# Turning four tiles of x by 16-bit transposing DMAs instead of on TensorE, with GpSimd splitting and interleaving the halves

## The chip, the cores and the metric

The kernel runs on one core of a Trainium2 chip. The metric is the device time of one execution in microseconds (us), lower is better. An engine here is one of TensorE (PE), VectorE (DVE), ScalarE (ACT), GpSimd (POOL) and SyncE (SP), which issues most transfers.

## The reference

Two graph layers over N = 1250 nodes with D = 512 features each, and a layer norm behind each of them. The graph has 21250 edges, sorted by destination.

```python
edge_index = stack([src, dst])
# first layer: hidden width 1024
agg = segment_sum(x[src], dst)
h = (1 + eps) * x + agg                       # called h0 below
h = relu(batch_norm(h @ W1 + b1))
h = relu(batch_norm(h @ W2 + b2))
x = layernorm(x + (x + h))
# second layer: hidden width 256
h = relu(x @ V1 + c1) @ V2 + c2
x = layernorm(x + h + segment_sum(h[dst], src))
```

All arrays are float32.

## The kernel before

The sum over edges is done as a matrix product with the adjacency counts A. x lies in SBUF as ten tiles of 128 rows (`xs[:, k, :]`, the last has 98 rows). A transposed copy `xT` (features on the partitions, nodes along the free dimension) is needed too, since `h0` is made with features on the partitions: `h0 = eps1 * xT + agg`. Large products are made exact enough by splitting each float32 operand in a high and a low part (`xh` and `xl` of x, `h0h` and `h0l` of h0, `wh` and `wl` of a weight).

**The stages around the change.** The transposed adjacency `AT` is built in NG = 25 groups of 50 destination nodes. For each group g, VectorE writes two sets of one-hot rows (`one_hots(g)`: `hot_s` with 1280 and `hot_k` with 500 bfloat16 elements per partition, each by comparing two operands that lie in SBUF), TensorE multiplies them (`build(g)`, ten small matmuls), and ScalarE copies the result from PSUM to `AT` (`group_out(g)`). The one-hot tiles have two buffers each: `one_hots(g)` waits until `build(g-2)` is done, and `build(g)` waits for `one_hots(g)` and for `group_out(g-2)`.

The nodes are aggregated in three chunks of columns, `CH = [(0, 250), (250, 750), (750, 1250)]`, which are complete behind groups 5, 15 and 25. From group 5 on TensorE does, in each slot g, `build(g)` and then four units of aggregation (`aggregate(i, k)`: two matmuls, of `xh` and `xl` of tile k). Slots 5 to 14 take chunk 0 (250 columns, one tile k = g - 5 in each slot), slots 15 to 24 take chunk 1 (500 columns), and chunk 2 follows as a tail. Tables set what else is done in a slot: `high_at` and `low_at` say behind which group `xh` (ScalarE) and `xl` (VectorE, `x_low`, again two operands in SBUF) of tiles 5 to 9 are made, `cols_at` says where TensorE turns tiles 7, 8 and 9 of x (`x_cols`: four transposes into a PSUM bank), and `turn_at` where ScalarE copies them to `xT` (`x_turn`). Tiles 5 and 6 are turned earlier, behind `build(2)` and `build(4)` (`early_cols`). `h0_own(i)` on VectorE adds `eps1 * xT` to the sums in PSUM, `h0_high` on ScalarE and `h0_low` on VectorE split the result.

GpSimd has nothing to do between the indirect loads at the start and the end of group 24. Then it makes the low parts of W1 (`wl`), which TensorE needs in the next stage, z = W1 h0. SyncE loads x, then W1, and then waits with the next transfers (`turns`, the spilled adjacency) for work behind group 24.

Later in the program the same machinery as in the change is used at another place: ScalarE writes the low and the high 16 bits of `xT` to two int16 planes, SyncE turns each of them by a transposing DMA (`plane_T<-planes`, 128x1280), and ScalarE and GpSimd write them back interleaved (`rows_back`).

Of the kernel before, what the change touches and what calls it, by code (L numbers as in the profile page):

```python
# [23 lines left out]
def gnn_kernel(nc, x, src, dst, eps, w1, b1, g1, be1, w2, b2, g2, be2, lw1, lb1, lw2, lb2, out, a_spill):  # L24
# [38 lines left out]
    with ctx:  # L63
# [116 lines left out]
        par_r = tmp("par_r", [P, P], F32)  # L180

# [72 lines left out]
        pads_set, bounds_set = sem("pads_set"), sem("bounds_set")  # L254
        rows_T, ln_var, ln_std_s, ln_aff, x1_last_set, x1_set = (
# [91 lines left out]
        cols_at = {6: half + 2, 7: half + 3, 11: half + 4}  # L347
        turn_at = {6: half + 2, 7: half + 3, 12: half + 4}
        high_at = {5: half, 8: half + 1, 9: half + 2, 10: half + 3, 11: half + 4}
        low_at = {7: half, 10: half + 1, 11: half + 2, 12: half + 3, 13: half + 4}  # L350
        early_cols = {EARLY - 3: half, EARLY - 1: half + 1}
        w1_at = {CHG[1] + t: t for t in range(HT)}
        assert EARLY == half and NT == half + 5 and max(cols_at) < CHG[1] and CHG[1] + HT <= NG and 2 + DT <= x_bank(half)
# [24 lines left out]
        def _(sp):  # L378
# [12 lines left out]
            for d in range(DT):  # L391
                sp.dma_start(w1s[:, :, d * P:d * P + P], w1[d * P:d * P + P, :].rearrange("p (t c) -> p t c", c=P)
                             ).then_inc(w1_in, 16)
            sp.wait_ge(pad_set, ATS)
# [42 lines left out]
        def _(pl):  # L437
# [25 lines left out]
            for t in half_out:  # L463
                nc.gpsimd.memset(t[:, N:COLS], 0).then_inc(pad_set, 1)
            pl.wait_ge(rowsel, 1)
# [9 lines left out]
            nc.gpsimd.memset(asked[0:1, :], 0.0).then_inc(runs_asked, 1)  # L475

# [77 lines left out]
        def _(act):  # L554
# [26 lines left out]
            def w1_high(t):  # L581
                if t == 0:
                    act.wait_ge(w1_in, 16 * DT)
                    act.wait_ge(xl_set, NT)
                    act.wait_ge(x_turned, NT)
                nc.scalar.activation(wh[:, t, :], w1s[:, t, :], ACT.Copy).then_inc(w1h_set, 1)
# [24 lines left out]
            with act.If(bad == 0):  # L611
                for g in range(EARLY, NG):
                    group_out(g)
                    if g in turn_at:
                        x_turn(turn_at[g])
# [9 lines left out]
            with act.Else():  # L625
                for k in turn_at.values():
                    x_turn(k)
# [168 lines left out]
        def _(v):  # L796
# [59 lines left out]
            def h0_own(i):  # L856
# [3 lines left out]
                if i == 0:  # L860
                    v.wait_ge(xT_set, NT)
# [4 lines left out]
            def h0_low(i):  # L866
                c, d = divmod(i, DT)
                c0, c1 = CH[c]
                v.wait_ge(h0h_set, i + 1)
                nc.vector.tensor_tensor(h0l[c][:, d, :], ps[:, 2 + i % 6, 0:c1 - c0],  # L870
# [276 lines left out]
        def _(pe):  # L1147
# [56 lines left out]
            def aggregate(i, k):  # L1204
# [3 lines left out]
                if k == 0:  # L1208
# [3 lines left out]
                    elif i >= DT:  # L1212
                        pe.wait_ge(xT_set, NT)
# [21 lines left out]
            with pe.If(bad == 0):  # L1235
                for g in range(EARLY, NG):
# [6 lines left out]
                    if g in cols_at:  # L1243
                        x_cols(cols_at[g])
            with pe.Else():
                for k in cols_at.values():
                    x_cols(k)
                pe.wait_ge(xT_set, NT)
# [173 lines left out]
```

## Time and profile before

| | |
|---|---|
| median of 3 runs | 249.57 us (249.5 to 250.74) |
| the profiled execution's own time | 249.95 us |
| its span from first to last instruction | 248.1 us |
| granted TensorE clock, mean | 0.995 |
| PE busy | 231.0 us (93%) |
| DVE busy | 156.2 us (63%) |
| ACT busy | 134.2 us (54%) |
| POOL busy | 88.0 us (35%) |

The span leaves 1.85 us of the execution's own time outside. Busy times are shares of the whole span; an engine can be idle on average and still be the one that is waited for in a stage.

### The profile page before, as it was taken

The page shows a single profiled execution, that of the slowest core. Times are in us where ns is not written, and L with a number is a line of the kernel's source. Part 1 is how long each engine was busy: PE and PEld are TensorE (multiplying, and loading weights), DVE is VectorE, ACT ScalarE, POOL GpSimd, SP SyncE. Part 2 cuts the span into 40 slices and gives each one's busy share as a digit, 9 for nine tenths or more (in the row PEclk, how much of TensorE's full clock was granted, in tenths as well). Part 3 has the DMA queues.
Part 4 walks back from the last instruction along what each step waited for, and adds up shares of the span by engine and source line. Part 5 has one row for each costly group of instructions (what it writes and reads, how often), then busy time and mean ns, then how long its engine had stood idle before and what let it go on. Part 6 is the DMA issues. An engine that isn't in the chain of part 4 may idle for free.

```text
span 248.1 us, 3897 instructions
## 1 busy us (share of the span) xinstructions
PE 231.0 (93%) x1454; PEld 197.3 (80%) x1454; DVE 156.2 (63%) x362; ACT 134.2 (54%) x233; POOL 88.0 (35%) x83
## 2 busy tenths in 40 slices
PE   0858999999999999999999999999999999999990
PEld 0845997777888888888888888888889997888970
DVE  1669899873966344555544316264876899796374
ACT  0656774763868067444455504457471639936373
POOL 5420000004920006565554500423456459701251
PEclk9999999999999999999999999999999999999998
DMA  3467800000066501111000087503209920000334
GB/s 100 156 214 214 202 0 3 1 3 3 3 261 239 198 1 45 42 42 45 0 0 0 4 206 142 106 3 60 45 4 170 202 85 3 0 0 0 131 127 160
DMA packets 32323, 19.96 MB, mean 80 GB/s; under 512 B 21927, under 2 KB 27084, under 8 KB 32302
## 3 DMA queue, kind: packets, MB, share of 16 engines
q1 hardware_dynamic: 31796, 19.45, 28.6%
q8 instruction: 13, 0.21, 0.4%
q0 software_dynamic: 160, 0.13, 0.2%
q10 hardware_dynamic: 346, 0.10, 0.2%
q14 instruction: 8, 0.07, 0.1%
HBM read 8.51 MB, written 5.92 MB: 58 GB/s over the span
## 4 chain that ended last, share of the span: by engine, by line
PE 70%; DVE 12%; DMA 7%; ACT 6%; issue 2%; POOL 1%; SPq 1%; DVEq 0%
PE ps L1281 22%; PE ps L1220 17%; PE ps L1298 11%; PE ps L1344 9%; PE ps L1362 6%; PE ps L1311 3%; DVE hot_s L849 3%; DMA plane_T<-planes 2%; PE ps L1200 2%; DMA src_i<-in_src 2%; DVE xT L984 2%; DMA pairs<-pair 2%; ACT planes L715 1%; DVE small_t L942 1%; DMA run<-pairs,start_i 1%
## 5 line engine op out<-in xcount | busy, mean ns | idle before, releaser
L942 DVE BATCH_NORM_STATS2 small_t<-ps 128x6 f32<-128x500 f32 (+1 forms) x36 | 21.6, 599 | 38.7 <-PE ps L1281 25.2
L1220 PE MATMUL ps<-AT,xh 128*128 128x500 f32 (+2 forms) x120 | 42.6, 366 | 0.4 <-ACT AT L569 0.4
L1220 PE MATMUL ps<-AT,xl 128*128 128x500 f32 (+2 forms) x120 | 40.9, 352 | 0.0
L1281 PE MATMUL ps<-h0h,wh 128*128 128x500 f32 (+1 forms) x96 | 33.9, 353 | 0.0
L1281 PE MATMUL ps<-h0h,wl 128*128 128x500 f32 (+1 forms) x96 | 33.9, 353 | 0.0
L1281 PE MATMUL ps<-h0l,wh 128*128 128x500 f32 (+1 forms) x96 | 33.8, 352 | 0.0
L485 POOL TENSOR_TENSOR wl<-w2s,wh 128x512 fp32r<-128x512 f32 x8 | 11.1, 1384 | 43.9 <-ACT wh L689 43.9
L480 POOL TENSOR_TENSOR wl<-w1s,wh 128x512 fp32r<-128x512 f32 x8 | 10.1, 1301 | 45.7 <-ACT AT L569 45.7
L1220 PEld LDWEIGHTS ps<-AT,xh 128*128 128x128 f32 (+1 forms) x120 | 22.6, 188 | 3.3 <-ACT AT L569 0.6
L1220 PEld LDWEIGHTS ps<-AT,xl 128*128 128x128 f32 (+1 forms) x120 | 22.7, 189 | 2.7
L1298 PE MATMUL ps<-a1h,wh 128*128 128x500 f32 (+1 forms) x96 | 23.7, 355 | 0.0
L1298 PE MATMUL ps<-a1h,wl 128*128 128x500 f32 (+1 forms) x96 | 23.5, 353 | 0.0
L1298 PE MATMUL ps<-a1l,wh 128*128 128x500 f32 (+1 forms) x96 | 23.4, 353 | 0.0
L569 ACT ACTIVATE AT<-ps 128x500 fp32r<-128x500 f32 x25 | 14.8, 590 | 15.6 <-PE ps L1200 15.6
L849 DVE TENSOR_TENSOR hot_s<-iota,loT 128x1280 bf16<-128x1280 bf16 x25 | 20.5, 820 | 2.3 <-PE ps L1200 2.2
L1344 PE MATMUL ps<-A,uh 128*128 128x512 f32 (+3 forms) x60 | 20.5, 357 | 0.0
L1281 PEld LDWEIGHTS ps<-h0h,wh 128*128 128x128 f32 x96 | 18.1, 188 | 2.9 <-issue 0.4
L1344 PE MATMUL ps<-A,ul 128*128 128x512 f32 (+3 forms) x60 | 20.3, 354 | 0.0
L1281 PEld LDWEIGHTS ps<-h0l,wh 128*128 128x128 f32 x96 | 18.0, 188 | 2.5
L1281 PEld LDWEIGHTS ps<-h0h,wl 128*128 128x128 f32 x96 | 18.0, 188 | 2.4
L489 POOL TENSOR_TENSOR a1l<-a,a1h 128x1250 fp32r<-128x1250 f32 x7 | 18.8, 2682 | 0.0
L663 ACT ACTIVATE small_t<-small_t 128x1 f32<-128x1 f32 x12 | 3.5, 295 | 27.7 <-DVE small_t L943 27.7
(148 smaller groups left out, 508.2 us busy)
## 6 DMA issues: line engine op xcount, KB each, us to landing
turns<-half_out SPq DMA_DIRECT2D x10, 320.0 KB, 2.2
out<-x SPq DMA_DIRECT2D x9, 256.0 KB
w1s<-in_L_gnn_W SPq DMA_DIRECT2D x4, 512.0 KB, 7.1
w2s<-in_L_gnn_W SPq DMA_DIRECT2D x8, 256.0 KB, 2.7
xs<-in_x SPq DMA_DIRECT2D x1, 1280.0 KB, 7.9
xs<-in_x SPq DMA_DIRECT2D x1, 1024.0 KB
lws<-in_L_gnn_W SPq DMA_DIRECT2D x1, 512.0 KB, 4.0
lw2s<-in_L_gnn_W SPq DMA_DIRECT2D x1, 512.0 KB, 4.2
```

Source lines behind the costliest of these rows:

```text
L480: nc.gpsimd.tensor_tensor(wl[:, t, :], w1s[:, t, :], wh[:, t, :].bitcast(F32), ALU.subtract).then_inc(w1l_set, 1)
L485: nc.gpsimd.tensor_tensor(wl[:, t, :], w2s[t % W2R][:, :], wh[:, t, :].bitcast(F32), ALU.subtract).then_inc(w2l_set, 1)
L489: nc.gpsimd.tensor_tensor(a1(a1l, t), a32[t % 2][:, :], a1(a1h, t).bitcast(F32), ALU.subtract).then_inc(a1l_set, 1)
L569: nc.scalar.activation(AT[:, :, g * WG * WIN:(g + 1) * WG * WIN].rearrange("p k (w d) -> p k w d", w=WG), ps[:, g % 2, 0:GCOLS].rearrange( ...
L849: nc.vector.tensor_tensor(hot_s[g % 2][:, :, :, :], iota2[:, None, :, :].broadcast_to([P, WG, P, 2]), loT[:, w, None, :].broadcast_to([P, ...
L942: link(nc.vector.bn_stats(stats[:, 6 * c:6 * c + 6], ps[:, zbank(t, c), 0:c1 - c0]))
L1220: last = mm(o, part[0:r, k, d * P:d * P + P], AT[0:r, k, c0:c1], start=(k == 0 and j == 0), stop=(k == NT - 1 and j == 1))
L1281: last = mm(ps[:, zbank(t, c), 0:c1 - c0], w[:, t, d * P:d * P + P], h[c][:, d, :], start=(d == 0 and j == 0), stop=(d == DT - 1 and j == 2))
L1298: last = mm(ps[:, zbank(t, c), 0:c1 - c0], w[:, k, (t - HT) * P:(t - HT + 1) * P], a1(a, k)[:, c0:c1], start=(k == 0 and j == 0), stop=(k ...
L1311: last = mm(u_at(k), x[:, d, P * k:P * k + r], w[:, d, :], start=(d == 0 and j == 0 and k % 2 == 0), stop=(d == DT - 1 and j == 2), skip_g ...
L1344: last = mm(v_at(i, m), (uh, ul)[j][0:r, k, m * P:m * P + P], a_rows(k)[0:r, c0:c1], start=(k == 0 and j == 0 and (m == 0 or v_banks[i][0] ...
L1362: last = mm(ps[0:r, y_banks[k % len(y_banks)], :], part[:, f:f + r], w[:, m, :], start=(m == 0 and j == 0), stop=(m == LT - 1 and j == 2))
```

## The change

Tile 5 is still turned on TensorE behind `build(2)`. Tiles 6 to 9 (XD = 6) are no longer turned on TensorE nor copied by ScalarE. Instead, GpSimd waits until group 10 is copied to `AT` (`AT_set` 11) and then copies the low and the high 16 bits of each float of tiles 6 to 8 (128x1536 int16 each) and of tile 9 (98x512 each) to two planes. SyncE issues two transposing DMAs from these planes (16 blocks of 128x128 each), SBUF to SBUF. GpSimd then interleaves the turned halves into `xT` in eight copies, two for each tile. The first `h0_own` of chunk 2 waits for them. The planes and their turned copies lie in 16 KB where `h0h` and `h0l` of chunks 1 and 2 are written later, so the last `h0_low` of chunk 1 waits for the DMAs, and ScalarE's write of `wh` tile 4, which lies over x tile 6, waits for the planes.

```diff
@@ the new tiles
+        XD = NT // 2 + 1
+        x_plane = [at(f"x_plane{i}", [P, NT - XD, D], I16, R_XD + i * (NT - XD) * XTILE) for i in range(2)]
+        x_plane_T = [at(f"x_plane_T{i}", [P, (NT - XD) * DT, P], I16, R_XD + (2 + i) * (NT - XD) * XTILE) for i in range(2)]
@@ the tables
-        cols_at = {6: half + 2, 7: half + 3, 11: half + 4}
-        turn_at = {6: half + 2, 7: half + 3, 12: half + 4}
+        x_parts = [(k0, k1, i) for k0, k1 in ((XD, NT - 1), (NT - 1, NT)) for i in range(2)]
+        PLANES_AT = 11
-        early_cols = {EARLY - 3: half, EARLY - 1: half + 1}
+        early_cols = {EARLY - 3: half}
@@ SyncE, behind the loads of W1
+            sp.wait_ge(x_plane_set, len(x_parts))
+            for i in range(2):
+                sp.dma_start_transpose(x_plane_T[i][:, :, :], x_plane[i][:, :, :].rearrange("p t d -> p (t d)")
+                                       ).then_inc(x_planes_T, 16)
@@ GpSimd, at its start
+            for t in x_plane:
+                nc.gpsimd.memset(t[:, NT - 1 - XD, :], 0).then_inc(x_pad, 1)
@@ GpSimd, ahead of its wait for group 24
+            def x_to_plane(k0, k1, i):
+                r = rows[k1 - 1]
+                nc.gpsimd.tensor_copy(x_plane[i][0:r, k0 - XD:k1 - XD, :], half_of(xs[0:r, k0:k1, :].rearrange(
+                    "p t d -> p (t d)"), i).rearrange("p (t d) -> p t d", d=D)).then_inc(x_plane_set, 1)
+
+            def x_late(k0, k1, i):
+                c0, c1 = P * k0, min(P * k1, N)
+                for k in range(k0, k1):
+                    r = rows[k]
+                    src = x_plane_T[i][:, (k - XD) * DT:(k - XD + 1) * DT, 0:r]
+                    out = xT[:, :, P * k:P * k + r].bitcast(I16).rearrange("p d (c i) -> p d c i", i=2)[:, :, :, i]
+                    last = nc.gpsimd.tensor_copy(out, src)
+                last.then_inc(xT_late, 1)
+
+            pl.wait_ge(x_in2, 32)
+            pl.wait_ge(x_pad, 2)
+            pl.wait_ge(AT_set, PLANES_AT)
+            for part in x_parts:
+                x_to_plane(*part)
+            for part in x_parts:
+                pl.wait_ge(x_planes_T, 32)
+                x_late(*part)
@@ ScalarE, in w1_high and behind group_out
-                    act.wait_ge(x_turned, NT)
+                    act.wait_ge(x_turned, XD)
+                if t == XD - X_UNDER_W1:
+                    act.wait_ge(x_plane_set, len(x_parts))
-                    if g in turn_at:
-                        x_turn(turn_at[g])
@@ VectorE, in h0_own and h0_low
-                    v.wait_ge(xT_set, NT)
+                    v.wait_ge(xT_set, XD)
+                if i == NI - DT:
+                    v.wait_ge(xT_late, len(x_parts))
+                if i == NI - DT - 1:
+                    v.wait_ge(x_planes_T, 32)
@@ TensorE
-                        pe.wait_ge(xT_set, NT)
+                        pe.wait_ge(xT_set, XD)
-                    if g in cols_at:
-                        x_cols(cols_at[g])
```

On TensorE the transposes stood between the aggregation of a slot and the next build. These are its rows in slots 6 and 7, before:

```order
L1220 MATMUL ps<-AT,xh 128x250
L1220 MATMUL ps<-AT,xl 128x250
L1162 MATMUL ps<-ident,xs 128x128 [waits xT_set,x_in2]
L1162 MATMUL ps<-ident,xs 128x128 x3
L1200 MATMUL ps<-hot_k_72,hot_s_70 128x50 [waits AT_set,hot]
L1200 MATMUL ps<-hot_k_72,hot_s_70 128x50 x9
L1220 MATMUL ps<-AT,xh 128x250 [waits xl_set]
```

And the same place of TensorE now:

```order
L1262 MATMUL ps<-AT,xh 128x250
L1262 MATMUL ps<-AT,xl 128x250
L1242 MATMUL ps<-hot_k_72,hot_s_70 128x50 [waits AT_set,hot]
L1242 MATMUL ps<-hot_k_72,hot_s_70 128x50 x9
L1262 MATMUL ps<-AT,xh 128x250 [waits xl_set]
```

Four transposes are gone here, and so they are behind the build of group 4, in slot 7 and in slot 11; each build follows the aggregation at once.

On GpSimd, between its last memset of the start and the first low part of W2, there stood before:

```order
L472 DMA run_113<-pairs,start_i_111 125x128 [waits start_set]
L475 MEMSET small_t 1x1
L480 TENSOR_TENSOR wl<-w1s,wh 128x512 [waits w1h_set,AT_set]
L480 TENSOR_TENSOR wl<-w1s,wh 128x512 [waits w1h_set] x7
L485 TENSOR_TENSOR wl<-w2s_53,wh 128x512 [waits w2h_set]
```

And now:

```order
L491 MEMSET small_t 1x1
L495 COPY x_plane_119<-xs 128x1536 [waits AT_set,x_pad,x_in2]
L495 COPY x_plane_120<-xs 128x1536
L495 COPY x_plane_119<-xs 98x512
L495 COPY x_plane_120<-xs 98x512
L504 COPY xT<-x_plane_T_121 128x4x128 [waits x_planes_T]
L504 COPY xT<-x_plane_T_121 128x4x128 x2
L504 COPY xT<-x_plane_T_122 128x4x128 [waits x_planes_T]
L504 COPY xT<-x_plane_T_122 128x4x128 x2
L504 COPY xT<-x_plane_T_121 128x4x98 [waits x_planes_T]
L504 COPY xT<-x_plane_T_122 128x4x98 [waits x_planes_T]
L519 TENSOR_TENSOR wl<-w1s,wh 128x512 [waits w1h_set,AT_set]
```

Twelve copies that read SBUF stand where GpSimd was idle; the low parts of W1 come behind them.

## Rows read from the trace of the kernel before

**Rows 1.** Windows of 7 and 21 us: busy us (instructions) of each engine, clock, DMA.

```profile
31.00:38.00 7.00, 6.74 (x93) 6.27 (x93) 7.00 (x13) 4.54 (x10) 0.00 (x0) 1.00 0.00 0
38.00:59.00 21.00, 21.00 (x182) 16.47 (x182) 16.47 (x33) 12.17 (x25) 0.00 (x0) 1.00 0.01 2
```

**Rows 2.** Chain that ended last, slots 5 to 14: start, us, what.

```profile
23.89 0.22 issue
...
26.82 0.44 PE ps L1162 x4
...
30.11 0.52 ACT xh L565
...
30.65 0.69 DVE xl L828
31.35 0.73 DVE hot_s L849
32.08 0.33 DVE hot_k L852
32.41 0.60 DVE xl L828
...
37.47 0.43 PE ps L1200 x10
```

**Rows 3.** Timeline: the copy of group 10 to AT, and tile 9's transposes.

```profile
31.88 0.59 ACT L569 ACTIVATE AT<-ps 128x500 fp32r<-128x500 f32 x1 [0.18 <-PE ps L1200]
...
33.99 0.50 PE L1162 MATMUL ps<-ident,xs 98*128 98x98 f32 x4
```

**Rows 4.** Groups by line on POOL: its int16 copies of the later stage.

```profile
L508 POOL COPY xr<-plane_T 128x640 int16<-128x640 int16 x6 | 5.3, 924 | 3.9 <-DMA plane_T<-planes 3.9
```

**Rows 5.** Timeline of POOL and DVE where both read SBUF, and alone.

```profile
168.04 1.21 DVE L994 TENSOR_TENSOR lws<-lws,ps 128x1024 f32<-128x1024 f32 x1
171.75 2.90 POOL L497 TENSOR_TENSOR xpl<-xT,xph 128x1250 fp32r<-128x1250 f32 x1 [8.15 <-ACT xph L706]
172.66 3.08 DVE L999 TENSOR_TENSOR lw1l<-lws,lw1h 128x1024 fp32r<-128x1024 f32 x1 [3.41 <-ACT lw1h L725]
...
67.14 1.34 DVE L963 TENSOR_TENSOR half_out<-half_out,ident 128x128 int16<-128x128 int16 x1
72.50 0.29 DVE L963 TENSOR_TENSOR half_out<-half_out,ident 128x128 int16<-128x128 int16 x1 [0.55 <-ACT half_out L639]
...
208.73 1.66 POOL L523 CAST A<-half_out 128x1250 fp32r<-128x1250 int16 x1
209.31 1.36 DVE L1065 SCALAR_TENSOR_TENSOR ul<-u,uh 128x256 fp32r<-128x256 f32 x1
```

**Rows 6.** The tile plane_T: time of an issue on SP in ns, time to landing.

```profile
L424 SPq DMA_TRANSPOSE plane_T<-planes x6: 1330/1442/1540, 156.8 to 186.2; - x6
...
DMA to landing us min/median/max: 3.5/3.5/5.5
```

**Rows 7.** One-hots of groups 19 and 20 on DVE, and the build of 20.

```profile
43.60 0.82 DVE L849 TENSOR_TENSOR hot_s<-iota,loT 128x1280 bf16<-128x1280 bf16 x1 [0.39 <-PE ps L1200]
...
47.35 0.41 DVE L852 TENSOR_TENSOR hot_k<-iota_k,keyT 128x500 bf16<-128x500 bf16 x1
...
49.81 0.28 PE ps L1200 x10
```

**Rows 8.** Timeline of POOL at the start.

```profile
6.83 1.18 POOL L466 IOTA nodes<- 128x1250 f32 x1 [2.35 <-DVE edge_row L812]
```

**Rows 9.** The low parts of W1 on POOL, and the chain's piece that uses them.

```profile
59.51 10.12 POOL L480 TENSOR_TENSOR wl<-w1s,wh 128x512 fp32r<-128x512 f32 x8 [45.72 <-ACT AT L569]
...
78.92 54.96 PE ps L1281 x288
```

**Rows 10.** Chain: TensorE's last work; and the window in which its clock falls.

```profile
234.07 8.40 PE ps L1362 x36
...
245.00:246.00 1.00, 0.00 (x0) 0.00 (x0) 0.39 (x1) 0.00 (x0) 0.00 (x0) 0.83 0.69 256
```

More of the change, by code:

```diff
@@ L180, in gnn_kernel @@
         par_r = tmp("par_r", [P, P], F32)
+        XD = NT // 2 + 1
+        XTILE = D * 2
+        R_XD = R_W - 4 * (NT - XD) * XTILE
+        x_plane = [at(f"x_plane{i}", [P, NT - XD, D], I16, R_XD + i * (NT - XD) * XTILE) for i in range(2)]
+        x_plane_T = [at(f"x_plane_T{i}", [P, (NT - XD) * DT, P], I16, R_XD + (2 + i) * (NT - XD) * XTILE) for i in range(2)]
+        assert TMP[0] <= R_XD and R_XD % 32 == 0
+        assert R_H0 + DT * (CH[1][0] + CH[1][1]) * 4 + (DT - 1) * (CH[1][1] - CH[1][0]) * 4 <= R_XD
+        assert R_H0 + 2 * DT * CH[2][0] * 4 <= R_XD + 2 * (NT - XD) * XTILE
         ident = misc("ident", [P, P], F32)
@@ L254, in gnn_kernel @@
         pads_set, bounds_set = sem("pads_set"), sem("bounds_set")
+        x_pad, x_plane_set, x_planes_T, xT_late = (sem(n) for n in ("x_pad", "x_plane_set", "x_planes_T", "xT_late"))
         rows_T, ln_var, ln_std_s, ln_aff, x1_last_set, x1_set = (
@@ L346, in gnn_kernel @@
         EARLY = CHG[0]
-        cols_at = {6: half + 2, 7: half + 3, 11: half + 4}
-        turn_at = {6: half + 2, 7: half + 3, 12: half + 4}
+        x_parts = [(k0, k1, i) for k0, k1 in ((XD, NT - 1), (NT - 1, NT)) for i in range(2)]
+        PLANES_AT = 11
         high_at = {5: half, 8: half + 1, 9: half + 2, 10: half + 3, 11: half + 4}
         low_at = {7: half, 10: half + 1, 11: half + 2, 12: half + 3, 13: half + 4}
-        early_cols = {EARLY - 3: half, EARLY - 1: half + 1}
+        early_cols = {EARLY - 3: half}
         w1_at = {CHG[1] + t: t for t in range(HT)}
-        assert EARLY == half and NT == half + 5 and max(cols_at) < CHG[1] and CHG[1] + HT <= NG and 2 + DT <= x_bank(half)
+        assert EARLY == half and NT == half + 5 and CHG[1] + HT <= NG and 2 + DT <= x_bank(half)
+        assert XD == half + 1 and CH[1][1] <= XD * P
         def h0_after(g):
@@ L625, in _ @@
             with act.Else():
-                for k in turn_at.values():
-                    x_turn(k)
                 for k in high_at.values():
@@ L1242, in _ @@
                         build(g)
-                    if g in cols_at:
-                        x_cols(cols_at[g])
             with pe.Else():
-                for k in cols_at.values():
-                    x_cols(k)
-                pe.wait_ge(xT_set, NT)
+                pe.wait_ge(xT_set, XD)
                 pe.wait_ge(gen_zero, 1)
```

## The prediction

> **What bounds the kernel now.** I read the chain that ended last first, since it says which engine each stretch waits for, and then the windows and timelines of the stretches that the change touches. TensorE holds most of the chain. The stretch in which the transposes stand is the exception. From 30.65 to 37.42 us the chain runs on VectorE alone: xl of a tile, hot_s, hot_k, again and again, at 0.60 to 0.69, 0.73 and 0.33 us apart, until the build of group 14 at 37.47 us can start [rows 2]. In the window from 31 to 38 us VectorE is busy 7.00 of 7.00 us, TensorE 6.74, and GpSimd does nothing [rows 1]. So both engines are nearly full there, and VectorE is the one that ends last. From 38 to 59 us it is the other way: TensorE is busy 21.00 of 21.00 us, VectorE 16.47 [rows 1]. The slots of that stretch take TensorE about 2.2 us each, while two one-hot instructions take VectorE 1.06 us.
>
> **What TensorE saves.** Four tiles are no longer turned. In slot 6 this is 0.44 us of the chain, and slot 7 has the same piece once more [rows 2]; tile 9 in slot 11 has 0.50 us [rows 3], and tile 6 behind group 4 counts as 0.44. That is 1.8 us of TensorE. But a build cannot start ahead of its one-hots, and VectorE's instructions are as many as before. What the saving can move is the start of VectorE's gapless run. It was released by xh of tile 6, which ScalarE made from 30.11 to 30.63 us, behind two copies of turned tiles [rows 2]; I put what VectorE waited for it at 0.1 us. The other place is the 0.22 us of issue at 23.89 us, ahead of the first aggregation [rows 2], where TensorE's sequencer comes from the transposes of tile 6. I take 0.3 us for both. The bounds are 0 and 1.8. ScalarE's four copies that go are not on the chain behind 30.65 us and give nothing more.
>
> **The four plane copies.** They are not in the trace. The nearest row is the same kind of copy, int16 with a step of two on one side, at 128x640: 924 ns [rows 4]; pairs of them take 1.75 us, 0.875 us each from start to start, as the row's busy time of 5.3 us over six also says. In proportion a copy of 1536 elements takes 2.1 us and one of 512 takes 0.7 us, 5.6 us for the four. Group 10 is copied to AT by 32.47 us [rows 3], so they start at about 32.2 us. This is inside VectorE's gapless run, with some 5 us of it to go.
>
> Do the two engines hold each other up? The trace has three kinds of places. At 171.75 us GpSimd works for 2.90 us on two SBUF operands, and a VectorE instruction with two SBUF inputs that starts at 172.66 takes 3.08 us, where one of the same shape with an input from PSUM takes 1.21 [rows 5]. It ends at 175.74, 1.09 us behind GpSimd's end: it did its work only when GpSimd was through. A 16-bit tensor_tensor takes 1.34 us beside GpSimd and 0.29 alone. A GpSimd cast with one input does the same: it ends at 210.39 and the VectorE instruction that started at 209.31 ends at 210.67 [rows 5]. The one-hots and xl all have two SBUF inputs. So each plane copy stops VectorE for nearly its own length. From the first pair, VectorE would have to begin 1.21 us ahead of 175.74, that is 0.12 us before GpSimd's end; I take 0.15 us off each copy: 1.95 + 1.95 + 0.55 + 0.55 = 5.0 us. VectorE has no idle time in the run to put this in, so the build of group 14 and all behind it moves by it. The bounds: 5.9 us if the copies cost in proportion to the 924 ns and hold the whole time, and 0 if GpSimd never gets in (a rival below).
>
> The Trainium skill, "SBUF — State Buffer", section "Who interferes with whom", speaks against this change: a VectorE instruction with two SBUF inputs and a GpSimd instruction that reads SBUF exclude each other, for the whole instruction, and issue order decides who waits. By its whole instruction the four would cost 5.6 us in place of 5.0. The rows above show the exclusion too, and the measured ends put it 0.1 us short of the whole.
>
> **The transposing DMAs.** An issue takes SP 1.44 us for 10 blocks, and its data land 3.5 to 5.5 us behind it [rows 6]. With 16 blocks in proportion: 2.3 us for the first issue, and 5.6 us behind the second; 7 us in all, with 5 and 8 as bounds. Behind the planes, which end at about 38.9 us (32.2, the 5.6 us of copies, and two or three VectorE instructions let in between), they land at about 46 us. SP has nothing else to issue until the adjacency is complete, so nothing is queued behind them.
>
> **The eight interleaving copies.** Six have 512 elements (0.7 us) and two 392 (0.54): 5.3 us, of which by the same 0.15 us they stop VectorE for 4.1. They fall on one-hots of groups 17 to 20. Before, hot_k of group 20 was done at 47.68 us and its build came at 49.81: 2.1 us of slack, and VectorE waited 0.39 us at 43.60 [rows 7], 2.5 us together. All this shifts by the same 4.7 us, so the slack stays. Two of the eight should fall on h0_own or h0_low, which have an operand in PSUM and are not stopped. Six times 0.55 less 2.5 is 0.8; I take 0.7. Bounds: 0 and 4.1 less 2.5, which is 1.6.
>
> **What costs nothing.** The two memsets of 128x512 at the start lie in front of a 2.35 us wait of GpSimd [rows 8]. The low parts of W1 come behind the interleaving; that is through at about 55 us, and the copy of group 24, for which they wait anyway, is at 59 plus the delay. They took 10.12 us from 59.51, and TensorE wants the first at 78.92 [rows 9], 9 us behind the last. The same slack covers h0_own of chunk 2, which waits for xT. ScalarE's wait for the planes stands in slot 19, some 10 us behind them.
>
> **The sum.** -0.3 + 5.0 + 0.7 = +5.4 us, on the profiled execution's 249.95 us: 255.35. The median before is 0.4 us under that execution, and I put the forecast at 255.2. Bounds of the terms: -1.8 to 0, 3.9 (copies a quarter cheaper than in proportion, still holding) to 5.9, 0 to 1.6; together 252.1 to 257.5. I hold the ends to be unlikely at once.
>
> **Rivals.**
> 1. TensorE's clock falls. With the copies in VectorE's way, hot_k of group 12 is done at 32.2 + 1.95 + 0.60 + 1.95 + 0.73 + 0.55 + 0.33 = 38.3 us, while TensorE is through with slot 11 at about 33.4: 4.9 us idle in one piece. At the end of the program TensorE's last work ends at 242.47, and the granted clock, 0.83 in the second from 245 on [rows 10], falls there from 2.4 to 1.2 GHz at about 245.66, after 3.2 us of idling. For: the gap is longer. Against: it is one gap, in a stretch that VectorE bounds. A slot of 1.3 us would take 2.6 against VectorE's 1.66, so 0.95 us lost in each of slots 12 to 14 at most, of which the wait hides the first: up to 1.5 us more, 255.5 to 256.8.
> 2. GpSimd is kept out, and the kernel is not slower. VectorE's instructions in the run overlap (820 ns long, 0.73 apart), and no row shows GpSimd getting in between two such. If it waits for VectorE's first idle time, that is at 43.60 us [rows 7], in TensorE's stretch: each copy then takes from a slack of 2 to 3 us and VectorE catches up before the next, the planes turn at about 57, xT is complete at about 70, and TensorE loses nothing or the tail waits up to 1 us: 249.6 to 250.7. It decides if the first plane copy ends behind 40 us. The rows where GpSimd stops VectorE are all ones in which GpSimd was there first.
> 3. These operands don't exclude each other, and only the saving is left: 249.65, or as little as 248.2 with all of TensorE's 1.8 us. The 16-bit and the one-input rows speak against it.
> 4. The reading with a step costs more than the writing with one, planes and interleaving half as dear again: 2.8 us more from the planes and up to 1.2 from the rest, 257 to 259. Nothing in the trace reads so.
>
> **How the numbers follow.** The forecast has 0.47, the clock 0.22, GpSimd kept out 0.15, no exclusion 0.07, dearer copies 0.09. Without the last rival's upper half, no exclusion and half of the case in which GpSimd is kept out, 0.8 is left: 250.2 to 258.4. A change of 0.5% (1.25 us) is about what a measurement can tell from none. Slower by more: 0.47 + 0.22 + 0.09 and nothing of the rest, 0.78. Faster by more: a part of the third rival, 0.04. Within: 0.18.
>
> **What the new profile would show.** Right: VectorE instructions of 2.0 to 2.8 us between 32 and 39 us where they were 0.4 to 0.8, the build of group 14 at 42 us, TensorE idle for 4 to 5 us in one piece at about 33 to 38, the transposes landed at about 46, no wait for xT or for wl. Wrong: a first plane copy that itself takes over 5 us (kept out), or hot_s staying at 0.82 us beside a plane copy. What I could have most wrong is the price of the copies, on which both positive terms of the sum hang.

## The result and the profile after

The changed kernel takes 251.25 us (median, 250.79 to 251.86) where the kernel before took 249.79 beside it: ratio 1.0052, 95% interval 1.0040 to 1.0065, or 1.3 us more. The forecast was 5.4 us more. The profiled execution took 251.40 us.

First GpSimd's timeline of the changed kernel:

```profile
32.68 11.67 POOL L495 COPY x_plane<-xs 128x1536 int16<-128x1536 int16 x4 [19.00 <-ACT AT L608]
51.96 7.01 POOL L504 COPY xT<-x_plane_T 128x512 int16<-128x512 int16 x8 [7.61 <-DMA x_plane_T<-x_plane]
60.31 10.10 POOL L519 TENSOR_TENSOR wl<-w1s,wh 128x512 fp32r<-128x512 f32 x8 [1.34 <-ACT AT L608]
```

VectorE's timeline of the same stretch:

```profile
37.51 0.81 DVE L887 TENSOR_TENSOR hot_s<-iota,loT 128x1280 bf16<-128x1280 bf16 x1
...
39.31 0.41 DVE L890 TENSOR_TENSOR hot_k<-iota_k,keyT 128x500 bf16<-128x500 bf16 x1
39.64 1.62 DVE L903 SCALAR_TENSOR_TENSOR ps<-xT,small_t,ps 128x250 f32<-128x250 f32 x4
41.19 1.95 DVE L887 TENSOR_TENSOR hot_s<-iota,loT 128x1280 bf16<-128x1280 bf16 x1
43.06 0.82 DVE L890 TENSOR_TENSOR hot_k<-iota_k,keyT 128x500 bf16<-128x500 bf16 x1
43.80 1.23 DVE L887 TENSOR_TENSOR hot_s<-iota,loT 128x1280 bf16<-128x1280 bf16 x1
```

The row of line 495, the plane copies, with the shortest, median and longest in ns:

```profile
L495 POOL COPY x_plane<-xs x4: 794/1330/8364, 32.7 to 43.6; 128x1536 int16<-128x1536 int16 x2, 98x512 int16<-98x512 int16 x2
```

The first plane copy "takes" 8.36 us, from 32.68 to 41.04, and the second 1.85. For 7 us the first did nothing: VectorE's one-hots keep their 0.81 and 0.41 us, and 12 of its instructions begin behind 32.68 and ahead of 39.64. It ends only when VectorE has come to `h0_own` (39.64), which has an operand in PSUM. The one-hots behind that become longer, but in the stretch where VectorE has slack [rows 1, 7].

The windows of the changed kernel, in the columns of [rows 1]:

```profile
31.00:38.00 7.00, 6.44 (x89) 5.76 (x87) 7.00 (x13) 4.12 (x8) 5.32 (x1) 1.00 0.01 2
38.00:45.00 7.00, 6.53 (x62) 5.22 (x59) 7.00 (x12) 3.40 (x7) 6.35 (x4) 1.00 0.01 2
45.00:60.00 15.00, 15.00 (x127) 11.58 (x126) 13.16 (x23) 9.02 (x19) 7.01 (x8) 1.00 0.44 72
...
79.00:90.00 11.00, 10.56 (x59) 8.91 (x58) 5.75 (x13) 3.50 (x7) 0.00 (x0) 1.00 0.54 185
```

TensorE loses 0.47 us at one build, at 43.93 (first line below), and nothing from 45 to 60 us, where the eight interleaving copies lie. But it stands again at 84.28 us, in the next stage, which no step of the prediction looked at. TensorE's waits in its timeline:

```profile
43.93 0.43 PE L1242 MATMUL ps<-hot_k,hot_s 128*128 128x50 bf16 x10 [0.47 <-DVE hot_k L890]
84.28 0.50 PE L1319 MATMUL ps<-h0h,wh 128*128 128x500 f32 x1 [0.43 <-DVE h0l L912]
```

ScalarE's timeline ahead of the second:

```profile
73.16 1.24 ACT L677 ACTIVATE half_out<-AT 128x1250 int16<-128x1250 f32 x1
...
75.57 1.25 ACT L677 ACTIVATE half_out<-AT 128x1250 int16<-128x1250 f32 x1 [1.08 <-DMA turns<-half_out]
76.72 0.18 ACT L677 ACTIVATION_READ_ACCUMULATOR half_out<-AT 128x1 f32 x1
76.81 0.57 ACT L635 ACTIVATE h0h<-ps 128x500 fp32r<-128x500 f32 x1
```

Behind group 24 ScalarE copies the ten tiles of counts to four buffers `half_out`, from which SyncE sends them to `turns`. The seventh copy reuses the third buffer and waits 1.08 us for the third transfer. Behind it on ScalarE stand `h0_high` of the second slice of chunk 2, the last three copies and `h0_high` of the third slice; VectorE and ScalarE then do the fourth slice, and TensorE waits for its `h0_low`. The chain says the same:

```profile
70.98 4.57 DMA turns<-half_out
75.55 0.02 issue
75.57 1.34 ACT half_out L677 x2
76.91 0.47 ACT h0h L635
77.38 3.68 ACT half_out L677 x6
81.06 0.48 ACT h0h L635
...
83.55 0.69 DVE h0l L912
...
84.28 51.10 PE ps L1319 x264
```

The row of `turns` gives its landing (min/median/max) as 2.2/4.2/5.5 us in the changed kernel; a second profile of the kernel before (e15) has 2.2/3.4/5.3 and no such wait. The change touches none of this code.

A part of what two profiles differ by is not the change. In e15, the kernel before again, TensorE's granted clock was 0.50 from 18 to 22 us and 0.78 from 22 to 24, where its first profile had 1.00, and group 24's aggregation began at 59.14 instead of 58.80. The changed kernel's profile had such a stretch too (0.50 from 22 to 24) and began it at 59.60. So 0.3 of the 0.8 us by which it looks late there is no more than two profiles of one kernel differ by. That the clock makes this difference is not shown: e9 (below), with a clock of 0.50 from 20 to 22, began its last build at 58.77, and e16, with full clock, at 58.97.

### The profile page after: what moved, and what is told of

It is laid out like the page before. It is cut to its first block, busy times and chain, and to the rows that moved or that the text cites. A ratio compares the mean times of both kernels' runs of the same rounds, so it can differ in the third digit from the quotient of the medians.

```text
span 249.5 us, 3876 instructions
## 1 busy us (share of the span) xinstructions
PE 231.2 (93%) x1438; PEld 196.6 (79%) x1438; DVE 160.4 (64%) x362; ACT 132.4 (53%) x229; POOL 107.4 (43%) x97
## 4 chain that ended last, share of the span: by engine, by line
PE 70%; DVE 15%; DMA 7%; ACT 5%; issue 2%; POOL 1%; SPq 0%; DVEq 0%; ACTq 0%
PE ps L1336 22%; PE ps L1319 20%; PE ps L1382 9%; PE ps L1262 7%; PE ps L1400 6%; DVE hot_s L887 5%; PE ps L1349 3%; DVE hot_k L890 2%; ACT half_out L677 2%; DMA turns<-half_out 2%; DMA src_i<-in_src 2%; DVE gains L1000 2%; PE ps L1242 2%; DMA pairs<-pair 2%; DMA run<-pairs,start_i 1%
## 5 line engine op out<-in xcount | busy, mean ns | idle before, releaser
L887 DVE TENSOR_TENSOR hot_s<-iota,loT 128x1280 bf16<-128x1280 bf16 x25 | 22.2, 888 | 1.2 <-PE ps L1242 1.1
L495 POOL COPY x_plane<-xs 128x1536 int16<-128x1536 int16 (+1 forms) x4 | 11.7, 2955 | 19.0 <-ACT AT L608 19.0
```

The lines of the kernel that those rows point to most:

```text
L495: nc.gpsimd.tensor_copy(x_plane[i][0:r, k0 - XD:k1 - XD, :], half_of(xs[0:r, k0:k1, :].rearrange("p t d -> p (t d)"), i).rearrange("p (t d ...
L887: nc.vector.tensor_tensor(hot_s[g % 2][:, :, :, :], iota2[:, None, :, :].broadcast_to([P, WG, P, 2]), loT[:, w, None, :].broadcast_to([P, ...
```

## The experiments

Ratios are to the kernel before on the same chip, with 95% intervals; 0.0010 is 0.25 us.

**e1, the saving alone.**

```diff
-    (wait for xs and AT; x_to_plane x4; x_late x4 on GpSimd; both transposing DMAs on SyncE)
+    nc.gpsimd.memset(xT[:, :, P * XD:N], 0.0).then_inc(xT_late, len(x_parts))
```

The waits of ScalarE and VectorE for the planes and the DMAs are left out with them.

> The changed kernel with its plane copies, both transposing DMAs and the eight interleaving copies left out: tiles 6 to 9 of xT are filled with zeros by one early GpSimd memset, so the output is not the reference's. It shows what TensorE and ScalarE save by themselves. By the forecast's first term 0.3 us less than before (249.5). A rival: the stretch up to the build of group 14 goes by VectorE alone, and the saving is nothing (249.8). A second rival: TensorE's emptier start lets its clock fall between 20 and 24 us, as in the profile of the changed kernel, and the time is 0.3 us above before (250.1).

Measured: 251.53 us, 1.0056 (1.0041 to 1.0071). With no plane, no DMA and no interleaving the whole loss is there. But the substitute disturbed the run; GpSimd's timeline of e1:

```profile
13.27 1.73 POOL L503 MEMSET xT<- 128x1928 f32 x1
```

VectorE's:

```profile
13.70 1.38 DVE L863 TENSOR_SCALAR rel<-run,small_t 125x128 f32<-125x128 f32 x1 [0.35 <-DMA run<-pairs,start_i]
```

In the kernel before this `rel` takes 0.29 us. The clearing held it, and the groups began 0.6 us late. ScalarE waited 0.80 for `turns` here too.

**e2, the additions alone.** TensorE and ScalarE turn all ten tiles again (`cols_at`, `turn_at`, `early_cols` of before restored), GpSimd and SyncE do their new work as well. The interleaving also waits for ScalarE's copies to `xT`, and ScalarE, VectorE and TensorE wait for ten turned tiles again. The main lines:

```diff
-        early_cols = {EARLY - 3: half}
+        early_cols = {EARLY - 3: half, EARLY - 1: half + 1}
+                    if g in turn_at: x_turn(turn_at[g])      # ScalarE
+                    if g in cols_at: x_cols(cols_at[g])      # TensorE
```

> All ten tiles are turned on TensorE as before, and GpSimd and SyncE do the plane copies, the DMAs and the interleaving of the changed kernel on top (the same values are written to xT once more). If the added part is what costs, this stands 1 to 1.5 us above before (250.8 to 251.3), the first plane copy ends at about 41 to 42 us and the build of group 17 comes some 0.6 us late. If the loss comes from what was taken off TensorE (its clock, its emptier slots), this is as fast as before (249.8). By the forecast's mechanism (each copy gets in at the next boundary) it would be above 254.

Measured: 254.53 us, 1.0189 (1.0165 to 1.0214). Here the planes got in at once. GpSimd's timeline of e2:

```profile
33.03 5.46 POOL L497 COPY x_plane<-xs 128x1536 int16<-128x1536 int16 x4 [19.33 <-ACT AT L611]
45.50 8.15 POOL L506 COPY xT<-x_plane_T 128x512 int16<-128x512 int16 x8 [7.01 <-DMA x_plane_T<-x_plane]
```

VectorE's:

```profile
33.33 2.08 DVE L893 TENSOR_TENSOR hot_s<-iota,loT 128x1280 bf16<-128x1280 bf16 x1
35.33 1.67 DVE L896 TENSOR_TENSOR hot_k<-iota_k,keyT 128x500 bf16<-128x500 bf16 x1
36.93 1.09 DVE L872 TENSOR_TENSOR xl<-xs,xh 128x512 fp32r<-128x512 f32 x1
37.95 1.23 DVE L893 TENSOR_TENSOR hot_s<-iota,loT 128x1280 bf16<-128x1280 bf16 x1
```

Against 0.82, 0.41, 0.68 and 0.81 undisturbed they are 1.26, 1.26, 0.41 and 0.42 longer, 3.35 us for the four copies. Group 24's aggregation began at 62.83, 3.7 behind e15's. There was no wait for `turns`, and the interleaving cost TensorE nothing: 15.00 busy of 15.00 from 45 to 60 us.

**e3, gaps in VectorE's run.** The changed kernel with a memset of two elements behind the one-hots of groups 11 to 14:

```diff
+                    if g in (11, 12, 13, 14):
+                        nc.vector.memset(gap[:, 2 * (g - 11):2 * (g - 11) + 2], 0.0)
```

> The changed kernel with four tiny VectorE memsets (no SBUF input), one behind the one-hots of each of groups 11 to 14. Theory A (an unbroken run of VectorE instructions with two SBUF inputs keeps the shared read port, and GpSimd gets in only at an instruction that does not need it): the first plane copy now ends at about 34 to 36 us in place of 41, the others follow at the next memsets, VectorE's one-hots behind them are stretched by 1 to 2 us, the build of group 14 comes at 40 to 42 us, and the time is 253 to 255. Theory B (the first copy's 8.4 us are its own cost, the engines don't exclude each other): the first copy still takes 8.4 us and the time stays at 251.2 to 251.6.

Measured: 254.71 us, 1.0179 (1.0153 to 1.0206). VectorE's timeline of e3, and GpSimd's:

```profile
32.43 0.06 DVE L929 MEMSET gap<- 128x2 f32 x1
33.01 2.09 DVE L888 TENSOR_TENSOR hot_s<-iota,loT 128x1280 bf16<-128x1280 bf16 x1
...
32.57 5.62 POOL L496 COPY x_plane<-xs 128x1536 int16<-128x1536 int16 x4 [18.80 <-ACT AT L609]
```

By its row the first memset was over 0.08 us before the plane copy came, and the copy got in at the next boundary; the pattern is that of e2. ScalarE waited 0.8 for `turns` here, so not all of the time belongs to the planes. The plane copies are the lever, and a break in VectorE's run just ahead of them lets them in.

**e4, planes behind group 19.** `PLANES_AT = 19`.

> The changed kernel with the planes behind group 18 instead of group 10 (PLANES_AT 19), so from about 47 us on, where TensorE is the bound and VectorE has idle time and 2 to 3 us of slack. Theory A: the copies get in at once, take some 6 us in all, no build waits for them, the transposed planes land at about 60 and the interleaving is through by 68 us, ahead of what waits for it: 249.8 to 250.3, the loss of 0.6 us at group 17 is gone. Theory B (a first copy of 8.4 us by its own cost): planes done at about 58, interleaving at about 75, h0_own of the last chunk and the low parts of W1 late, 251 to 254.

Measured: 250.72 us, 1.0029 (1.0015 to 1.0042), lower than the changed kernel but above before, and a miss for the 249.8 to 250.3 of theory A. The copies got in at once, but one build waited 0.53 for its one-hots at 50.53. The interleaving now lies at 59.16 to 64.5 and pushes `wl` to 64.42, the packet of e9 below passed at 73.0, and TensorE waited 1.21 at 85.14.

**e5 and e8, the order of the copies,** in the kernel before and in the changed one:

```diff
-        halves = [range(0, 4), range(4, 7), range(7, NT), range(0)]
+        halves = [range(0, 4), range(4, 6), range(6, NT), range(0)]
```

> The kernel before with one edit: the copies of the counts of tiles to half_out are split 4, 2, 4, 0 between the four high parts of chunk 2 instead of 4, 3, 3, 0, so that the seventh copy, which has to wait for the third transfer to turns, stands behind h0_high of the second slice and no longer ahead of it. In the kernel before, that copy waits for nothing, so both theories expect no change here, 249.5 to 250.1: it is the control for e8. If it is faster or slower by more than 0.4, the order itself has a price, and e8 has to be read against it.

> The changed kernel with the edit of e5. There the seventh copy waits 1.08 for the third transfer to turns, h0_high of the second slice of chunk 2 stands behind it, and TensorE waits 0.43 for h0_low. Theory C: with the high part ahead of the copy TensorE no longer waits there: 0.4 to 0.7 less than the changed kernel, 250.5 to 250.9. Rival E: the wait is covered by TensorE's queue or comes back one slice later at the eighth copy: 251.1 to 251.4.

Measured: e5 250.25 us, 0.9996 (0.9983 to 1.0009), nothing. e8 250.52 us, 1.0012 (0.9999 to 1.0026), 1.0 less than the changed kernel by the ratios. ScalarE still waits for `turns`, 0.39, but nobody behind it does: TensorE is busy 11.00 of 11.00 from 79 to 90 us. So the wait was worth 0.5 to 1.0 us of the 1.3 (this run and e9).

**e6 and e7, the saving with the clearing elsewhere.** In e6 the memset stands behind `AT_set` of group 24, ahead of `wl`; in e7 moreover tile 6 is turned on TensorE, and only tiles 7 to 9 are cleared (from `P * (XD + 1)` on):

```diff
+            pl.wait_ge(AT_set, NG)
+            nc.gpsimd.memset(xT[:, :, P * XD:N], 0.0).then_inc(xT_late, len(x_parts))
-        early_cols = {EARLY - 3: half}
+        early_cols = {EARLY - 3: half, EARLY - 1: half + 1}      # e7 only
```

> As e1 (TensorE no longer turns tiles 6 to 9 and nothing takes the work over; xT of tiles 6 to 9 is only cleared), but GpSimd's clearing of xT stands behind group 24, ahead of wl, instead of ahead of the planes at 13.3. Theory C: the 1.4 of e1 come from leaving the transposes out (later start of the run of VectorE behind the gap of TensorE, and the wait for turns in ScalarE's seventh copy): 251.0 to 251.6 again. Rival D: the early clearing held up VectorE, and e1 overstated it: then 249.6 to 250.5, and the 1.3 of the whole change come from the planes and the interleaving after all.

> As e6, but TensorE and ScalarE turn tile 6 behind build 4 as in the kernel before; tiles 7 to 9 alone are left out. It asks which of the transposes was worth something to the time. If the gap of TensorE behind build 4 and its clock at 20 to 24 carry the loss, this is back at 249.5 to 250.2. If the loss comes from the transposes inside the slots of groups 6, 7 and 11 (their saving lets the rest run ahead, into transfers that land late), it stays with e6, near 251.3.

Measured: e6 251.34 us, 1.0047 (1.0028 to 1.0066); e7 251.38, 1.0041 (1.0022 to 1.0060). They can't be read as intended. The memset pushed `wl` back by 1.7 us in e6 and by 1.3 in e7, onto more of VectorE's int16 additions to `half_out` (three took 3.96 and 3.94 us where the changed kernel's took 2.83), the packet of e9 below passed late in both (70.5 and 72.0), and TensorE waited 1.22 and 0.39 behind them. Their ratios differ by less than their intervals, so they show nothing of tile 6 either.

**e9 and e10, code that is not executed.** What e1, e4, e8 and the changed kernel share against before, e2 and e5 is the time at which a packet of instructions passes. The queues in the DMA view of the changed kernel from 72.5 to 73.0 us (packets, MB, share of 16 engines):

```profile
q1 hardware_dynamic: 75, 0.19, 95.4%
q8 instruction: 1, 0.02, 15.6%
```

The same view of e15 from 64.5 to 65.0:

```profile
DMA packets 1, 0.02 MB, mean 33 GB/s; under 512 B 0, under 2 KB 0, under 8 KB 0
...
q8 instruction: 1, 0.02, 16.3%
```

15.6% of 16 engines for 0.5 us is one engine held for 1.25 us, among transfers that keep all the others busy. In e15 it passes 4 us ahead of the first transfer, alone. The edit puts matmuls in the branch that is not taken:

```diff
             with pe.Else():
+                between(28)      # e9, changed kernel; between(100) in e10, kernel before
```

> The changed kernel with 28 matmuls written into the Else branch of TensorE, which is not taken: nothing more is executed, only the instructions behind the branch lie 56 instructions further on, where they lay in the kernel before (28 transposes left the program, 16 of them executed, 12 in that Else). In the traces a packet of instructions (16 KB, 1.2 to 1.6 on one of the 16 DMA engines) passes at 63.5 to 64.5 in the kernel before and e5 and at 67.5 in e2, ahead of the transfers to turns, but at 72.5 in the changed kernel and at 72 to 73 in e1, e4 and e8, between them, and only there does the third transfer land 4.2 to 4.6 after its issue. Theory F: this packet delays the third transfer, and with it ScalarE's seventh copy (1.08) and TensorE (0.43 and a restart). Then the packet is back near 64, the wait for turns is gone, and the time is 250.3 to 250.8. Rival G: the late landing has another cause (the phase of the transfers against ScalarE's copies): packet moved, wait still there, 251.1 to 251.5.

> The kernel before with 100 matmuls in the Else branch of TensorE, not taken: 200 instructions, so that the packet boundaries behind the branch come 200 instructions earlier, which is 56 short of a whole packet of 256. Nothing else is changed. Theory F: the packet that passed at 93.5 now passes near 72, one of the first transfers to turns lands above 4 after its issue, ScalarE's seventh copy waits 0.5 to 1.1 for it, and the kernel before loses 0.4 to 0.9: 250.5 to 251.0 on this chip if before is 250.1. Rival G: unchanged within 0.2.

Measured: e9 250.74 us, 1.0032 (1.0019 to 1.0044). The packet passed at 64.5, landing was 2.2/3.3/5.2, nobody waited for `turns`, and TensorE was busy 11.00 of 11.00 us from 79 to 90. e10: 252.01 us, 1.0087 (1.0070 to 1.0105), more than theory F gave, and for another reason. The packet came at 73.0, but 4.7 us behind the first transfer, and no copy waited. Instead TensorE stood at the jump; its timeline in e10:

```profile
60.12 0.38 PE L1220 MATMUL ps<-AT,xl 98*128 98x500 f32 x1
61.98 0.47 PE L1220 MATMUL ps<-AT,xh 128*128 128x500 f32 x1 [1.48 <-DVE h0l L870]
```

The same place in e15:

```profile
60.66 0.39 PE L1220 MATMUL ps<-AT,xl 98*128 98x500 f32 x1
60.89 0.39 PE L1220 MATMUL ps<-AT,xh 128*128 128x500 f32 x1
```

The matmul at 61.98 is the first behind the If. The row names `h0l` as releaser, but in e15 the same matmul starts at 60.89, while that `h0l` starts at 61.74. So it did not wait for that `h0l`. That it waited for its instructions is argued only: the packet before the stand came at 59.2 and took about 1.2 us, the next came at 62.5, and none passed during the stand. The other 0.7 of the 2.2 us of e10 stays unplaced.

**e11 and e13, the saving again, padded.** e11 is e1 with `between(28)`; in e13 the clearing moreover waits for the twentieth group:

```diff
+            pl.wait_ge(AT_set, 20)
             nc.gpsimd.memset(xT[:, :, P * XD:N], 0.0).then_inc(xT_late, len(x_parts))
```

> As e1 (transposes of tiles 6 to 9 left out, nothing in their place, xT of these tiles cleared early), with the 28 matmuls of e9 in the Else branch. Theory F: e1's loss of 1.4 was mostly the packet: 0.7 to 1.0 less than e1, 250.4 to 250.8 where before is 250.1; what remains is the later start of VectorE's run. It does not get faster than before by more than 0.3, since VectorE bounds groups 10 to 17 and TensorE's freed time there is slack. Rival G: as e1, 251.5.

> As e11 (transposes of tiles 6 to 9 left out with nothing in their place, xT of these tiles only cleared, 28 matmuls in the Else branch of TensorE), but the clearing stands behind the twentieth group. In e1 and e11 it ran at 13.27 and held VectorE's rel for 1.38 instead of 0.29, so that every group started 0.55 late, and in e6 it pushed wl by 1.7 into VectorE's work on half_out. If the saving by itself is worth nothing but costs nothing (VectorE bounds the groups), this is within 0.3 of before: 249.7 to 250.3 where before is 250.0. If leaving the transposes out has a cost of its own, it stays at 250.7 or more.

Measured: e11 251.12 us, 1.0048 (1.0034 to 1.0063), a miss for theory F: the wait for `turns` was gone, but the groups began 0.8 late behind the early clearing. e13 250.02 us, 0.9990 (0.9981 to 0.9999). Without the early clearing the loss is gone, and the saving is worth 0.25 us, between 0.02 and 0.5; e15, the unchanged kernel measured as one more version, came out at 0.9995.

**e12, an attempt at the best version.** `PLANES_AT = 19`, the split of e8, `between(28)`.

> An attempt at the best version: the changed kernel with PLANES_AT = 19, where VectorE has idle time and TensorE does not wait for it, the split of e8, and the 28 matmuls of e9 in the Else branch. Theories A and F together: the plane copies cost TensorE nothing (group 24 as early as in the kernel before or 0.1 to 0.3 earlier), no wait for turns: 249.6 to 250.3, within 0.3 of before. If it is slower than before by over 0.5, a third cost is still unnamed.

Measured: 251.02 us, 1.0041 (1.0026 to 1.0055), a miss. GpSimd's timeline of e12:

```profile
58.82 5.32 POOL L504 COPY xT<-x_plane_T 128x512 int16<-128x512 int16 x8 [7.14 <-DMA x_plane_T<-x_plane]
64.08 10.24 POOL L519 TENSOR_TENSOR wl<-w1s,wh 128x512 fp32r<-128x512 f32 x8
```

VectorE's:

```profile
66.68 3.93 DVE L1005 TENSOR_TENSOR half_out<-half_out,ident 128x128 int16<-128x128 int16 x3
```

The late planes push the interleaving against `wl` and `wl` onto the additions, as in e6, and one build waits 0.52 at 50.11; TensorE waits 0.36 more at 83.87. No version here beats the kernel before.

**e14, planes earlier, and e15, before again.** e14: `PLANES_AT = 8` and `between(28)`. e15: no edit.

> The changed kernel with PLANES_AT = 8 and the 28 matmuls of e9. GpSimd may begin its first plane copy some 3 us earlier. Theory A (VectorE's unbroken run keeps GpSimd out until its first instruction that reads PSUM, h0_own near 39.5): the copy begins earlier but ends at the same place, 40.5 to 41.2, as one instruction of about 11 to 13, and the time is that of e9 within 0.3. If instead the copy ends early in the run of VectorE, the exclusion depends on who waited first, and the time goes up by 2 to 4 as in e3.

> The kernel before, unchanged, as one more kernel of the comparison: a second profile of it, and a measure of what the comparison calls no difference. Ratio 0.998 to 1.002. TensorE's granted clock may be at half speed somewhere between 19 and 24, as in e5 and e2, or at full speed as in the first profile; if so, the 0.3 to 0.4 by which e5 and the changed kernel start their groups later does not belong to the change.

Measured: e15 250.07 us, 0.9995 (0.9985 to 1.0005). e14 254.09 us, 1.0150 (1.0136 to 1.0165), against theory A: GpSimd came at 28.21 and got in at once, in an unbroken run. VectorE in e14:

```profile
27.52 0.82 DVE L887 TENSOR_TENSOR hot_s<-iota,loT 128x1280 bf16<-128x1280 bf16 x1
28.25 1.69 DVE L890 TENSOR_TENSOR hot_k<-iota_k,keyT 128x500 bf16<-128x500 bf16 x1
29.87 2.08 DVE L887 TENSOR_TENSOR hot_s<-iota,loT 128x1280 bf16<-128x1280 bf16 x1
```

**e16, both remedies:** the split and `between(28)` in the changed kernel.

> The changed kernel with both remedies for the wait for turns, the split of e8 and the 28 matmuls of e9, PLANES_AT as it was. If both only remove the same wait, this is what either gives, 250.3 to 250.8 where before is 250.0; what is left above before then belongs to the plane copies behind 41. If they add up, 249.8 to 250.2.

Measured: 250.85 us, 1.0023 (1.0012 to 1.0033). They don't add up; they remove the same wait.

**e17 and e18, where the copy comes.** Both with `between(28)`; e17 has `PLANES_AT = 10`, e18:

```diff
             pl.wait_ge(AT_set, PLANES_AT)
+            pl.wait_ge(xh_set, half + 4)
```

> The changed kernel with PLANES_AT = 10 and the 28 matmuls of e9. e14 and e2 have refuted theory A as it stood: there GpSimd got in although VectorE's run was unbroken. What the nine traces have in common is where in VectorE's instruction the first plane copy comes: 0.15 to 0.17 behind the start of xl in the changed kernel, e8, e9 and e16 (kept out for 7 us), 0.31 behind it in e2 and 0.69 behind the start of hot_s in e14 (in at the next boundary). Theory H: a copy that comes just behind the start of a VectorE instruction is kept out until the run breaks, one that comes later in it gets in at the next boundary. With PLANES_AT = 10 it comes at about 31.4 minus the 0.2 to 0.4 by which these kernels differ, 0.54 behind the start of xl: in at once under theory H, first copy 1.7 to 2.1, hot_s near 31.4 takes 2.0, and the time is 253.5 to 254.5. Theory A: kept out for 8 us, first copy 9.5 to 10, 250.5 to 250.9.

> The changed kernel with the 28 matmuls of e9, in which GpSimd waits, behind AT of the eleventh group, for the high part of x as well (ScalarE's xh, which ends 0.51 later). The first plane copy then comes at 33.2 minus the same 0.2 to 0.4, some 0.08 behind the start of hot_s. Theory H: just behind the start of an instruction, so it is kept out again until h0_own near 39.3: one copy of 7.5 to 8, 250.5 to 250.9. If it gets in at once here (hot_s or hot_k of 1.7 to 2.1, 254), the place in the instruction does not decide, and why the changed kernel is spared stays open.

Measured: e17 250.49 us, 1.0014 (1.0002 to 1.0026); e18 250.63, 1.0023 (1.0009 to 1.0036). GpSimd's timeline of e17:

```profile
31.68 12.97 POOL L495 COPY x_plane<-xs 128x1536 int16<-128x1536 int16 x4 [17.81 <-ACT AT L608]
```

Of e18:

```profile
32.62 11.16 POOL L495 COPY x_plane<-xs 128x1536 int16<-128x1536 int16 x4 [18.93 <-ACT xh L605]
```

Both were kept out. In e17 the copy came 0.54 behind the start of xl, late in it, so theory H falls; theory A's numbers for e17 came true (a first copy of 9.66 us), though e2 and e14 speak against it as it stood. What fits all nine traces is how long VectorE had then run without a break (a start more than 0.03 us behind the usual distance): 1.3 us in e14, 2.0 in e2, 0.1 in e3 behind its memset, and GpSimd got in; 4.3 us in e17 and 5.6 to 6.2 in the changed kernel, e8, e9, e16 and e18, and it was kept out. That was found in the traces afterwards, and no run was made to test it.

## Why the prediction was wrong, by its steps

**The failed step** is the four plane copies: that each gets in at once and that "VectorE has no idle time in the run to put this in", 5.0 us. They did not get in: the first stood from 32.68 to 41.04, and the four together cost TensorE 0.47 us at one build (0.8 by the ratios, below) in place of 5.0. The second half is right where the copies do get in: e2, e3 and e14 lost 3.75 to 4.7 us. What happened is rival 2, given 0.15: the first copy ended behind the 40 at which the rival said it decides, and both signs that the prediction gave for being wrong came, a first copy of over 5 us and `hot_s` at 0.82 us beside it. The rival's own time, 249.6 to 250.7, was too low for the changed kernel (251.25); it had no wait for `turns` either. That the measured time still lies in the stated range, 250.2 to 258.4, is owed to the part that the range took in of this rival, not to the sum. GpSimd was let in not at VectorE's first idle time (43.60 before) but at its first instruction with an operand in PSUM. The Trainium skill, "SBUF — State Buffer", section "Who interferes with whom", says that whoever issues first gets the shared ports for its whole instruction, and that issue order decides who waits. The long one-hots beside plane copies agree with the exclusion. The order does not: in the changed kernel the copy was there at 32.68, and 12 VectorE instructions that started later went ahead of it. The measurement decides.

**Its size, had the step held,** was too high as well: 3.35 us by VectorE's rows in e2 for 5.0. One copy costs 1.26 and not 1.95, the small ones 0.41 and not 0.55. The row that I scaled from writes with a step of two; these read with it, and whether that is the reason no run shows. e14 paid 3.75 by its ratio, e2 4.7, in which TensorE's clock has a part: 0.78 from 38 to 45 us, a fall of the clock as in rival 1, in small.

**TensorE's saving,** -0.3: borne out, -0.25 in e13, with an interval of -0.5 to -0.02. VectorE's run now goes on without a break at the xl of 30.84, where VectorE had waited 0.12 us before.

**The interleaving,** +0.7: too high. With TensorE busy 15.00 of 15.00 from 45 to 60 us in the changed kernel and in e2, it costs nothing there. In the changed kernel it fell on the one-hots of groups 22 to 24 and not on 17 to 20, and four of them were 0.3 to 0.5 us longer, 1.8 in all where 4.1 was forecast. Where it is pushed to 59 us it does cost (e4, e12), through `wl` and VectorE's additions behind it; of `wl` the prediction had asked only when TensorE wants the first.

**The transposing DMAs, the memsets and the late waits** cost nothing, as said: landing in 4.3 to 5.1 us, all interleaved by 59 us. From the end of the planes to the landing it took 7.6 us. The recorded 7 does not add up from its own terms, 2.3 and 5.6, which give 7.9.

**A missing term,** +0.8: the wait for `turns`. Five versions without TensorE's wait (e8, e9, e16, e17, e18) have ratios of 1.0012 to 1.0032, mean 1.0021; the changed kernel has 1.0052. The difference is 0.0031, or 0.8 us. From e13 to that mean is again 0.0031, 0.8 us. I put it down to the plane copies in TensorE's stretch, of which the rows show 0.47 at one build; the rest, 0.3 us, is placed by no row. So -0.25 + 0.8 + 0.8 = 1.35. That this meets the 1.3 measured is no check, since each term is the difference of one ratio to the next. The intervals are 0.25 us or more to either side, so the split is no better than that. The traces put the wait for `turns` lower: from the start of the last build to the end of the span, without the 0.43 us for which TensorE stands at 84.28, the changed kernel takes 189.9 us, e9 190.0, e16 189.8 and before 189.7. By them the wait is worth 0.43 us, the low end of the 0.5 to 1.0 by the ratios.

Shown: that undoing the wait in two independent ways (order of copies, unexecuted code) takes off 0.5 to 1.0 us by the ratios, and that the versions without it are still not faster than before. Shown too is that the packet's time follows the code ahead of it in the program (72.5 to 64.5 by 28 matmuls and their weight loads that never run) and that the wait goes with it. Argued only: that the packet itself delays the third transfer, by holding one of 16 engines for 1.25 us. The wait of 1.08 has that size, and a fast landing (median 3.0 to 3.5) goes with a packet ahead of the first transfer in before, e2, e5, e9 and e11 to e18, a slow one (3.7 to 4.2) with a packet behind it in the changed kernel, e1, e3, e4, e6, e7 and e8; e10 is the case where it came later and hurt nobody. Open is the rule by which VectorE keeps GpSimd out.

## What to carry to other kernels

Where two engines were seen to hold each other up, ask of an instruction not only what it costs inside but whether it gets in, and look at where it then lands. A small change of the program can also cost at a place that it does not touch: compare the time at which instruction packets pass, and test with code that is never executed before a difference of half a per cent is put down to the change itself. A substitute in an "only this part" experiment must be shown not to disturb: three of the experiments here (e1, e6, e11) measured their own memset.

## What the runs showed of the hardware that was not expected

- VectorE, in a run of instructions with two SBUF operands and no break for 4.3 us or more, kept a waiting GpSimd copy out for 6.4 to 8.2 us; it was let in when VectorE came to an instruction with an operand in PSUM. Behind a break of 0.07 to 0.12 us 1.3 and 2.0 us earlier (e14, e2), or a memset of 0.06 us just ahead of it (e3), it was let in at the next boundary.
- Code that is not executed changes the time: 200 instructions in an untaken branch cost 2.2 us (e10), 1.48 of it as a stand of TensorE behind the jump that the profile puts down to VectorE. The packets are 0.02 MB. The Trainium skill, "Advanced Engine Details and Errata", section "ISA Cache", gives the line of the instruction cache as 16 KB or 256 instructions. The size agrees; no run here measured a period of 256.
- An int16 copy of 1536 elements that reads with a step of two lengthens the VectorE instruction beside it by 1.26 us (e2). Its own row there has 1.70 us, of which up to 0.37 is a wait for VectorE's xl, which it met under way.
- A GpSimd memset of 1.73 us, which reads nothing, held a one-input VectorE `tensor_scalar` for 1.1 us (e1).
- TensorE's granted clock was at half (1.2 GHz) for 3 us or more between 16 and 24 us in most of these profiles, of both kernels, and at full in others (the first profile of before, e16 and e18 among them).
